# First attention layer: the mask of the natural scores moves from a TensorE matmul to a VectorE add-and-maximum

## The reference, cut to what matters

```
q = apply_rope(proj(Wq, bq)) * Dh ** (-0.5)
k = apply_rope(proj(Wk, bk))
scores = jnp.einsum('bhqd,bhkd->bhqk', q, k)
blocked = (rel > 0) | (rel < -WINDOW)          # rel = key - query, WINDOW = 128
scores = jnp.where(blocked[None, None], -jnp.inf, scores)
probs = jax.nn.softmax(scores, axis=-1)
```

## Time and profile before

| | before |
|---|---|
| median of 3 executions | 2615.41 us (2611.98 to 2615.44) |
| the profiled execution, its own time | 2620.68 us |
| its span | 2618.8 us |
| PE / DVE / ACT / POOL busy, share of the span | 84% / 55% / 38% / 34% |
| mean granted TensorE clock | 0.939 of full |
| first attention layer in the trace | about 0 to 1070 us |

### The profile page before, as it was taken

The page is one execution under the profiler, slowest core; times in us unless marked ns, Lnnn a source line. Parts: engine busy times, 40 slices in busy tenths (PEclk is TensorE's granted clock), DMA queues, the critical chain, the costliest instruction groups (busy, mean ns, idle before and its releaser), DMA issues.

```text
span 2618.8 us, 42567 instructions
## 1 busy us (share of the span) xinstructions
PE 2206.4 (84%) x17140; PEld 1381.4 (53%) x17140; DVE 1430.5 (55%) x2527; ACT 994.5 (38%) x1449; POOL 899.5 (34%) x573
## 2 busy tenths in 40 slices
PE   2899999999999999588678689999378888888885
PEld 1444555555555555466556546776255555555553
DVE  2445554555555554446456445544566776677672
ACT  0133333333333333345334333334034554554443
POOL 4112222222222220103122122201338777877784
PEclk7799999999999999799989899999679999999997
DMA  6555555555556550456685841101454454446411
GB/s 132 101 113 115 106 122 106 106 116 113 114 111 118 111 108 26 147 193 246 227 287 190 285 137 65 49 19 55 138 140 109 125 156 128 128 105 165 120 44 49
DMA packets 226386, 328.86 MB, mean 126 GB/s; under 512 B 14368, under 2 KB 163984, under 8 KB 225936
## 3 DMA queue, kind: packets, MB, share of 16 engines
q1 hardware_dynamic: 219200, 321.56, 46.9%
q10 hardware_dynamic: 6992, 4.60, 0.6%
HBM read 197.53 MB, written 127.93 MB: 124 GB/s over the span
## 4 chain that ended last, share of the span: by engine, by line
PE 29%; DVE 12%; POOL 6%; DMA 5%; ACT 3%; issue 2%; SPq 1%; ACTq 0%; DVEq 0%; POOLq 0%
DVE l1f_rowmax L1785 4%; PE l1a_slot L1407 4%; POOL l1f_added L1665 4%; PE l1a_slot L1449 2%; PE l1a_slot L1398 2%; POOL l1f_added L1667 2%; PE l0f_slot L1108 2%; PE l1f_slot L1916 2%; DMA l0f_wide<-expert_outputs 2%; PE l0f_slot L1115 2%; PE l1f_os L1840 2%; PE l1f_slot L1907 2%; DMA l0f_x<-x 2%; DMA expert_outputs<-l0f_wide 1%; PE l0f_slot L1122 1%
## 5 line engine op out<-in xcount | busy, mean ns | idle before, releaser
L530 ACT ACTIVATE l0a_probs<-l0a_slot 128x1024 f32<-128x1024 f32 (+1 forms) x256 | 248.6, 972 | 335.9 <-PE l0a_slot L690 188.6
L587 DVE TENSOR_REDUCE l0a_rowmax<-l0a_slot 128x4 f32<-128x1024 f32 (+1 forms) x256 | 293.5, 1156 | 130.7 <-PE l0a_slot L700 127.8
L1735 ACT ACTIVATE l1f_probs<-l1f_slot 128x1024 f32<-128x1024 f32 x240 | 244.0, 1023 | 274.2 <-PE l1f_slot L1916 267.7
L1665 POOL TENSOR_TENSOR l1f_added<-l1f_probs 128x1024 f32<-128x1024 f32 x117 | 277.5, 2372 | 155.7 <-ACT l1f_probs L1735 155.7
L1785 DVE TENSOR_REDUCE l1f_rowmax<-l1f_slot 128x1 f32<-128x1024 f32 x240 | 287.3, 1217 | 66.8 <-PE l1f_slot L1907 66.3
L490 POOL TENSOR_TENSOR l0a_turned<-l0a_turned 128x512 f32<-128x512 f32 x32 | 40.8, 1274 | 557.9 <-DVE l0a_turned L573 557.9
L1916 PE MATMUL l1f_slot<-l1f_Qs,l1f_Ks 128*128 128x256 f32 x960 | 173.0, 304 | 37.9 <-DVE l1f_lo L1775 14.8
L1907 PE MATMUL l1f_slot<-l1f_Ks,l1f_Qs 96*128 96x512 f32 x480 | 177.9, 457 | 27.2 <-DVE l1f_rowmax L1785 18.1
L1916 PEld LDWEIGHTS l1f_slot<-l1f_Qs,l1f_Ks 128*128 128x128 f32 x960 | 145.3, 196 | 95.8 <-DVE l1f_rowmax L1785 32.7
L690 PE MATMUL l0a_slot<-l0a_mask,l0a_ident 128*128 128x512 bf16 (+1 forms) x512 | 150.3, 376 | 25.7 <-issue 23.3
L632 PE MATMUL l0a_O<-l0a_probs,l0a_V 128*32 128x128 f32 x3840 | 156.7, 279 | 11.2 <-issue 11.2
(11 more groups left out here) (193 smaller groups left out, 4015.0 us busy)
## 6 DMA issues: line engine op xcount, KB each, us to landing
expert_outputs<-l0f_wide SPq DMA_DIRECT2D x64, 512.0 KB, 3.3
l0f_wide<-expert_outputs SPq DMA_DIRECT2D x32, 1024.0 KB, 11.4
l0a_Qs<-qk_rows SPq DMA_DIRECT2D x96, 256.0 KB, 7.8
l0a_Ks<-qk_rows SPq DMA_DIRECT2D x96, 256.0 KB, 14.6
l1f_Ks<-kq_rows SPq DMA_DIRECT2D x48, 512.0 KB, 8.3
l0f_f<-in_dram SPq DMA_DIRECT2D x10, 2048.0 KB, 15.5
qk_rows<-l0a_hi SPq DMA_DIRECT2D x32, 512.0 KB, 2.8
qk_rows<-l0a_lo SPq DMA_DIRECT2D x32, 512.0 KB, 4.2
```

Of the source, the lines that this page charges most:

```text
L530: exp_ready.by(act.activation(probs[:, t % 2, HG * g:HG * g + HG, 0:reach, :], s[:, :, 0:reach, :], ACT.Exp, scale=SCALE))
L587: max_ready.by(dve.reduce_max(rowmax[:, t, :, 2 * g:2 * g + 2], s[:, :, :, first:2 * P], AX))
L1665: halved.by(pool.tensor_tensor(added[:, u, :], probs[:, 0, u, :], probs[:, 1, u, :], ALU.add))
L1735: exp_done.by(act.activation(probs[:, half, u - FIRST[b], :], s[:, :], ACT.Exp, scale=SCALE))
```

## The change

TensorE no longer adds the mask in a `nat` step; its first product of each half now starts the accumulation. In place of one `reduce_max` over the slot, DVE runs four `tensor_tensor_reduce` instructions, one for each head. Each adds the mask table (bf16, in SBUF) to that head's 256 scores in PSUM, writes the sums back to the same place in PSUM, and gives the maximum (starting from -3e38) to one column of `rowmax`. Only the last of the four signals `max_ready`. Scale and start value are immediates. The turned form is computed as before.

```diff
+    LOWEST = -3e38
...
+        visible = mask[:, :, :].rearrange("p a n -> p (a n)")
...
-                    max_ready.by(dve.reduce_max(rowmax[:, t, :, 2 * g:2 * g + 2], s[:, :, :, first:2 * P], AX))
+                    for half in range(2):
+                        for j in range(2):
+                            scores = s[:, half, j, first:2 * P]
+                            last = dve.tensor_tensor_reduce(scores, scores, visible[:, first:2 * P], 1.0, LOWEST, ALU.add, ALU.max,
+                                                            rowmax[:, t, half, 2 * g + j:2 * g + j + 1])
+                    max_ready.by(last)
...
-                    mask_ends = bool(kind == "tr" and g % 2)
+                    mask_begins, mask_ends = kind == "tr" and g % 2 == 0, kind == "tr" and g % 2 == 1
...
                             at_end = mm(o[:, half, :, reach, :], ident16[:, :],
-                                        table[:, reach, :].unsqueeze(1).broadcast_to([P, 2, wide, P]),
-                                        start=not mask_ends, stop=bool(mask_ends), skip_group_check=True)
+                                        maskT[:, reach, :].unsqueeze(1).broadcast_to([P, 2, wide, P]),
+                                        start=mask_begins, stop=mask_ends, skip_group_check=True)
...
-                    if not mask_ends:
+                    if mask_begins:
                         add_mask()
...
-                                      right[r, 2 * g + j, moving], start=mask_ends and not j, stop=not mask_ends,
+                                      right[r, 2 * g + j, moving], start=kind == "nat" or (mask_ends and not j), stop=not mask_ends,
```

More of the change, by code:

```diff
@@ L678, in piece @@
                         reach = slice(0 if tile else 1, 2)
-                        rows, table, left, right = ROWS, mask, Qs, Ks
+                        rows, left, right = ROWS, Qs, Ks
                         moving = slice(P * (tile - 1 + reach.start), P * tile + P)
@@ L682, in piece @@
                         reach = slice(0, 2 if tile < NT - 1 else 1)
-                        rows, table, left, right = ROWS + 1, maskT, Ks, Qs
+                        rows, left, right = ROWS + 1, Ks, Qs
                         moving = slice(P * tile, P * (tile + reach.stop))
                     wide = reach.stop - reach.start
-                    mask_ends = bool(kind == "tr" and g % 2)
+                    mask_begins, mask_ends = kind == "tr" and g % 2 == 0, kind == "tr" and g % 2 == 1
                     def add_mask():
```

## The result

The changed kernel takes 2726.8 us (median of 4, 2723.7 to 2734.1) against 2615.4 (2612.0 to 2616.3): ratio 1.0432, 95% interval 1.0409 to 1.0456. The forecast was 2701 with a range of 2605 to 2820: slower, as said, by 111 us where 86 were forecast.

What follows compares the result with a forecast made beforehand. It took four DVE reductions in a row, with TensorE's list queued behind maxT, as the bound. A longer chain (+36 us) and clock falls (+50) made +86 on the median 2615.4: 2701 us, range 2605 to 2820.

Steps and rivals of the forecast that it cites:

- What binds the layer: First attention layer: TensorE's list queues behind maxT, which waits for the last of four DVE reductions in a row.
- u: Time one new DVE instruction over 256 columns takes in a row, put at 0.41 us; balance zero at 0.375.
- the bounds: Limits for one new DVE instruction: 0.334 us if the maximum is free, 0.583 if each half waits for the other.
- The tile sums: Shift of maxT by kind of tile from the longer DVE chain: 4.5 us per two blocks, +36 us in all.
- The clock: TensorE idles 2.4 us before maxT, and its clock falls to 1.2 GHz behind most such waits: +50 us.
- 40 waits x 7/9: Long waits at maxT in 40 of 64 tiles, seven in nine followed by a clock fall costing 1.5 us: 47 us.
- nine stretches: TensorE idle stretches of 2.0 to 2.5 us in the layer's tail and last layer; the clock fell behind seven.
- Slots, DVE behind `maxT`: Waits for slots and DVE's work behind the four maxima: claimed to add nothing to the sum.
- ACT's `place`: ACT's issue of place, left about 11 us instead of 13 before the next tile's first tr step.
- u = 0.334: Rival: the maximum comes free from the same DVE instruction; -42 us, or 2573 to 2590 with some clock drops; chance 0.12.
- u = 0.50: Rival: the DVE instruction's two halves don't overlap; 128 us plus 70 for the clock, some 2813; chance 0.16.
- the clock that holds: Rival: DVE chain as forecast but TensorE's clock stays up; +36 us, 2651; chance 0.18.

Runs made afterwards that it cites:

- e6: Changed kernel with DVE masking only in every second nat step, TensorE masking and one reduction in the others: 2587.1 us, ratio 0.9899 to the kernel before.
- e7: Changed kernel with DVE masking only in the first nat step of a tile, TensorE in the other three: 2599.4 us, ratio 0.9924 to the kernel before.
- e1: Changed kernel with TensorE's mask put back in the nat steps, DVE's work as changed: 2663.8 us, ratio 1.0165 to the kernel before.
- e3: Kernel before without the natural mask, its single reduction kept, the copy of the turned maxima halving them: 2580.9 us, ratio 0.9854.
- e11: Kernel before with the last nat step of each tile reduced three times by DVE, adding 2.36 us of work ahead of maxT: 2833.7 us, ratio 1.0825.
- e2: Changed kernel with the matmuls of each tile's first tr step done three times over: 2713.5 us, ratio 1.0358 to the kernel before.
- e4: Changed kernel with the large piece and second tr step moved ahead of maxT for i = 1, 2, 3: 2742.7 us, ratio 1.0461 to the kernel before.
- e8: Changed kernel with the masked scores written to an unused SBUF tile instead of PSUM: 2664.0 us, ratio 1.0174 to the kernel before.

## Why the prediction was right, and where its sizes were off

- **What binds the layer** (four reductions in a row and `maxT` behind them, not DVE's free half): right; e6 and e7 came out by that rule, e1 within 4 us once its own starts are put in, and e3 showed how little of TensorE's saving could arrive.
- **u**: 0.382 for 0.41, 28 us too much. Two errors partly cancelled, which was luck: what was put at 0.074 for the maximum's own instruction is 0.011, and the write to PSUM, left inside the bounds without a term, costs 0.037. The bounds held.
- **The tile sums**: with the measured u they give maxT at 7.35, 7.90, 9.0 and 6.9 for i = 2, 3 and the two i = 1; the trace has 7.40, 7.85, 9.02 and 6.88. For i = 0 the prediction read one tile, with a pv of 16, and gave its gain to all. In every second one pv steps are half as long, `maxT` was not at 7.66 but at 6.79, the products behind it at 7.47 (483.42 - 475.95), where they still are after the change, so nothing was gained:
```profile
475.95 0.42 PE L632 MATMUL l0a_O<-l0a_probs,l0a_V 128*32 128x128 f32 x8 [0.58 <-issue]
...
482.74 0.27 PE L706 MATMUL l0a_slot<-l0a_ident,l0a_rowmax 128*16 128x128 f32 x1
483.42 0.50 PE L700 MATMUL l0a_slot<-l0a_Qs,l0a_Ks 49*128 49x256 f32 x4 [0.40 <-ACT l0a_probs L530]
```
  The chain costs 15 us, where 36 were forecast and the same sum with the measured u gives 8.
- **The clock**: the mechanism was right, its term mis-sized, 50 us where about 93 are. The price of a stretch was near (1.5 us forecast, 1.6 measured, in the change as in e11, though many are 6.8 us long). The count was not: 40 waits x 7/9 are 31 stretches, and the layer has 52 more than before. In the steady part all 30 tiles of the kinds it had counted hold a fall, not seven in nine, and so do 11 of 12 with i = 0, where shorter waits follow one another and to which it gave none. Its nine stretches also left out the feed-forward layer, where three waits of 2.45 us began at full clock and one was followed by a fall; the share differs from place to place (1 in 6 behind 1.8 us in e1), and what decides it is open.
- **Slots, DVE behind `maxT`**: they added nothing to the chain, as said. **ACT's `place`**: its DMA was late once in the steady part (1.7 us) and twice in the layer's opening (5.3 and 3.0 us, at 99 and 116 us), where the kernel before does not wait for it; that its reserve is nearly used up showed fully when tiles or the order changed (e2, e3, e4).
- **The rivals**: u = 0.334 and u = 0.50 are out by the trace, the clock that holds by the granted 0.86. The chain was forecast 21 us too dear and the clock 43 us too cheap, so the total came nearer than its parts: it is 25 us short.

## What to carry to other kernels

A busy share says which engine could be relieved, not whether the relief arrives: find the step at which the bound engine's in-order list waits for the other engine, and move work only as far as both reach it together. Here a half of the change gains 1.0%, the whole loses 4.3%. When an engine that was never idle starts to wait, price the clock behind the wait as well as the wait; here it was about six times the chain's own cost. And put a trial in front of the small transfers that ride behind large ones.

## What the runs showed of the hardware that was not expected

- An add with a running maximum takes DVE 0.345 us per 256 columns with its output in SBUF and 0.382 in PSUM (e8 and the change); a plain two-input add from PSUM to SBUF 0.334.
- TensorE's granted clock fell in all 24 tiles of the change that wait 1.9 to 2.2 us at `maxT` (i = 2 and 3), and stayed at half rate for 3.4 or 6.8 us in most of them though the work behind was dense. In e1 a wait of 0.77 us brought none in 13 tiles, one of 1.04 us in 3 of 7 and one of 1.8 us in 1 of 6; but 11 of 12 tiles with i = 0 in the change hold a fall, with waits of mostly 0.3 to 1.0 us close behind one another.
